# Two attention blocks of sixteen 8-feature heads, packed four side by side into TensorE's tiles

## The reference

```
scores = q @ k.T * 8 ** -0.5        (128 x 128; the fifth block adds a causal mask)
out    = softmax(scores) @ v        (128 x 8)
x      = x + concat(out) @ Wo + bo
```

## Time and profile before

| | us |
|---|---|
| median of 3 runs | 1275.42 (1272.52 to 1280.17) |
| the profiled execution | 1274.87 |
| its span | 1273.1 |
| first block, from the query product to the first scores | 10.57 to 49.25 |
| its head loop, to the turn of tokens | 49.25 to 129.14 |
| fifth block, from the product with `Wqkv` to the first scores | 383.18 to 418.46 |
| its head loop, to the turn of tokens | 418.46 to 539.45 |

### The profile page before, as it was taken

One profiled execution on the slowest core, in us unless ns is written; L12 is line 12 of the kernel. 1 busy time (PEld: TensorE's weight loads), 2 busy tenths in 40 slices (PEclk: granted clock), 3 DMA queues, 4 the chain that ended last, 5 costly groups with the idle time before them and its releaser, 6 DMA issues.

```text
span 1273.1 us, 18672 instructions
## 1 busy us (share of the span) xinstructions
PE 1145.1 (90%) x7950; PEld 769.5 (60%) x7950; DVE 549.3 (43%) x952; ACT 488.7 (38%) x755; POOL 423.3 (33%) x194
## 2 busy tenths in 40 slices
PE   7999798998989999988878986999999999999558
PEld 4898543673676788825556873655565565565334
DVE  2234466114436433354233334445554544553444
ACT  2355532433435544524343203444334434443111
POOL 0144111001000455401001000778677678677000
PEclk9799899996778999979997997999999999999769
DMA  8322100003000233210045102122123113110100
GB/s 338 128 101 117 51 33 34 1 1 148 34 15 19 88 130 133 117 67 33 17 194 220 67 14 119 67 91 108 67 68 132 67 66 133 67 67 1 72 1 9
DMA packets 20772, 102.96 MB, mean 81 GB/s; under 512 B 1744, under 2 KB 1744, under 8 KB 18896
## 3 DMA queue, kind: packets, MB, share of 16 engines
q1 hardware_dynamic: 20688, 101.75, 20.8%
HBM read 67.93 MB, written 33.82 MB: 80 GB/s over the span
## 4 chain that ended last, share of the span: by engine, by line
PE 83%; DVE 7%; ACT 5%; issue 2%; POOL 2%; DMA 0%; POOLq 0%; DVEq 0%; ACTq 0%
PE PSUM L2122 18%; PE PSUM L2048 10%; PE PSUM L1529 8%; PE PSUM L1662 4%; PE PSUM L1653 3%; PE PSUM L1539 3%; PE PSUM L1581 3%; PE PSUM L1618 3%; PE PSUM L1759 2%; PE PSUM L1770 2%; PE PSUM L1612 2%; PE PSUM L1714 2%; PE PSUM L2165 1%; PE PSUM L1981 1%; PE PSUM L1971 1%
## 5 line engine op out<-in xcount | busy, mean ns | idle before, releaser
L470 POOL TENSOR_TENSOR CK<-CK,ARENA 128x2048 f32<-128x2048 f32 x63 | 285.1, 4526 | 123.3 <-ACT ARENA L770 119.2
L2122 PE MATMUL PSUM<-ARENA,CT 128*128 128x512 f32 x512 | 238.7, 606 | 0.0
L1370 DVE TENSOR_TENSOR ARENA<-PSUM,RK 128x512 f32<-128x512 f32 x256 | 159.0, 684 | 183.8 <-PE PSUM L2048 183.8
L770 ACT ACTIVATE ARENA<-ARENA,WB 128x1024 f32<-128x1024 f32 x128 | 147.0, 1148 | 200.9 <-DVE ARENA L1370 198.2
L2122 PEld LDWEIGHTS PSUM<-ARENA,CT 128*128 128x128 f32 x512 | 91.4, 189 | 98.6 <-issue 90.5
L2048 PEld LDWEIGHTS PSUM<-ARENA 64*128 64x128 f32 x2048 | 119.4, 188 | 51.0 <-issue 47.0
L1529 PE MATMUL PSUM<-CT,WK 128*128 128x128 f32 x1024 | 144.6, 288 | 0.0
L1529 PEld LDWEIGHTS PSUM<-CT,WK 128*128 128x128 f32 x1024 | 129.8, 199 | 12.1 <-issue 8.7
L2048 PE MATMUL PSUM<-ARENA 64*128 64x128 f32 x2048 | 131.8, 278 | 2.7 <-ACT WB L765 2.2
L399 POOL TENSOR_TENSOR RSTD<-VE,MHALF 128x4 f32<-128x4 f32 x17 | 17.1, 1008 | 344.9 <-DVE VE L845 282.1
L413 POOL TENSOR_TENSOR W<-KEYS 128x512 f32<-128x512 f32 x28 | 36.8, 1314 | 126.5 <-ACT KEYS L493 92.6
(11 more groups left out here) (390 smaller groups left out, 1670.7 us busy)
## 6 DMA issues: line engine op xcount, KB each, us to landing
ARENA<-kept_keys SPq DMA_DIRECT2D x16, 2048.0 KB, 7.9
kept_keys<-KEYS SPq DMA_DIRECT2D x32, 512.0 KB, 2.6
kept_keys<-W SPq DMA_DIRECT2D x32, 512.0 KB, 2.6
CT<-in_ctxT SPq DMA_DIRECT2D x4, 1024.0 KB, 10.7
CK<-in_l0f_experts SPq DMA_DIRECT2D x1, 4096.0 KB, 22.5
CK<-in_ctxk SPq DMA_DIRECT2D x1, 4096.0 KB, 12.3
ARENA<-in_l2f_experts SPq DMA_DIRECT2D x2, 2048.0 KB, 7.8
CT<-in_ctxk SPq DMA_DIRECT2D x1, 4096.0 KB, 14.1
```

The lines of the kernel that those rows point to most:

```text
L470: nc.gpsimd.tensor_tensor(LS[b % 2], LS[b % 2], PR[:, t % 2, :], ALU.add)\
L770: act(p, p, ACT.Exp, bias=SHIFT).then_inc(sem("l3x_probs"), AC.sends("l3x_probs"))
L1370: ve.tensor_tensor(PR[:, k, q * 512:(q + 1) * 512].rearrange("p (j n) -> p j n", j=4), bank(q).rearrange("p (j n) -> p j n", j=4), each(rk ...
L2122: last = mm(bank(4 + q), CTK[:, t, :], PR[:, t % 2, q * 512:(q + 1) * 512], start=k == 0, stop=k == KEY_TILES - 1)
```

## The change

It changes both blocks in the same way.

- Heads lie in the array's quarters. Head j of a group has its 8 features in partitions 32j to 32j+7 for queries (`QH`) and keys (`KVH`), and its values in the 8 partitions behind. The four score products of a group use four row tiles and go to four banks (0 to 3), all of which the next group needs again: scores(g+1) waits until group g has been shifted.
- The product with the exponents is turned round: the 32-wide weights are the values, 8 columns that count, and a column of ones (`VH`) that gives the sum of the exponents. Four column tiles side by side fill a slice of bank 6; VectorE copies the bank every four groups (`keep_values`), so its sums (`total`) go. After the loop TensorE turns the kept values (`turn_values`, 16 transposes) and `normalize_heads` divides, with one reciprocal and one product for each batch element.
- Queries, keys and values are made by column-tiled products with 32-wide weights: in the first block 16 of 512 columns for the queries and 64 of 128 for keys with values; in the fifth 128 of 128 columns, whose moving operand is read in runs of 8 tokens. The masked copies of the queries, the transposes by heads, and the copies of 8 partitions go. Values get to rows by 16 transposes, and ScalarE copies them (`keep_value_rows`).
- GpSimd clears `VH` (2048 columns) and sets its ones ahead of each block (`value_pads`), directly behind the norm's power.
- The transposed exponents have one bank (4). A key tile has two banks where it had three: rows in 5 and 7, the sums of the tile before in 5 behind its first half of rows, the norms two tiles back in 7 ahead of its second half. The order of a tile is: turn norms of s-2, rows half 0, rows half 1, sums of s-1.
- The weights of the first block no longer wait for the array `wb`; `l3x_pick` has moved to `wa`.

```diff
-        VS = SM[:, 512:1024]
+        QH, KVH, VH, OH32 = (ARENA[:, k * 2048:(k + 1) * 2048] for k in range(4))
...
+            def value_pads():
+                nc.gpsimd.memset(VH, 0.0).then_inc(sem("value_pads"), PO.sends("value_pads"))
+                nc.gpsimd.wait_ge(sem("value_pads"), PO.sent("value_pads"))
+                nc.gpsimd.memset(VH.rearrange("p (h x) -> p h x", x=32)[:, :, 16:17], 1.0)\
...
+            def heads_act(place, scale):
+                first = places[place][0]
+                def begin(s):
+                    if s > first and s >= 2:
+                        keep_key_norms(s - 2, 7)
+                    keep_key_rows(s, 0, 5)
+                def end(s):
+                    if s:
+                        keep_key_sums(s - 1, 5)
+                for g, (one, two) in enumerate(key_steps(place)):
+                    nc.scalar.wait_ge(sem("scores_shifted"), AC.due("scores_shifted"))
+                    act(SX[:, g % 2, :], SX[:, g % 2, :], ACT.Exp, scale=scale).then_inc(sem("probs"), AC.sends("probs"))
...
+                        begin(one)
+                    if two is not None:
+                        keep_key_rows(one, 1, 7)
+                        end(one)
+                    nc.scalar.wait_ge(sem("probs_turned"), AC.due("probs_turned"))
...
+                    act(PT[:, g % 2, :], bank(4), ACT.Copy).then_inc(sem("pt_ready"), AC.sends("pt_ready"))
+                    if two is not None:
+                        begin(two)
+                        keep_key_rows(two, 1, 7)
+                        end(two)
+                    elif one is not None:
+                        keep_key_rows(one, 1, 7)
+                        end(one)
...
+            def normalize_heads():
+                for b in range(B):
+                    o = bank(b).rearrange("p (h x) -> p h x", x=32)
+                    nc.vector.wait_ge(sem("values_turned"), DV.due("values_turned"))
+                    ve.reciprocal(L_INV[:, b * H:(b + 1) * H], o[:, :, 16]).then_inc(sem("dve_step"), DV.sends("dve_step"))
+                    nc.vector.wait_ge(sem("dve_step"), DV.sent("dve_step"))
+                    last = ve.tensor_tensor(ACC[:, b, :].rearrange("p (h e) -> p h e", h=H), o[:, :, HD:2 * HD],
+                                            each(L_INV[:, b * H:(b + 1) * H], HD), ALU.mult)
...
+            for k in range(8):
+                rows_of = (QH, KVH)[k // 4].rearrange("p (c j) -> p c j", j=H)[:, :, 4 * (k % 4):4 * (k % 4) + 4]
+                bias = w(("l1a_bq", "l1a_bkv")[k // 4])[:, 4 * (k % 4):4 * (k % 4) + 4]
+                nc.vector.wait_ge(sem("kv_rows"), DV.due("kv_rows"))
+                ve.tensor_tensor(rows_of, bank(k).rearrange("p (j c) -> p c j", j=4), over(bias, P), ALU.add)\
...
                     for j in range(4):
-                        last = mm(PSUM[:, 1 + g % 2, j * P:(j + 1) * P], q_of(g, j), k_of(g, j), start=True, stop=True)
+                        r = slice(32 * j, 32 * j + HD)
+                        last = mm(PSUM[:, j, 0:P], q_of(g, r), KVH[r, g * P:(g + 1) * P], start=True, stop=True)
...
+                def begin(s):
+                    if s > first and s >= 2:
+                        nc.tensor.wait_ge(sem("keys_kept"), 2 * s)
+                        turn_norms(s - 2, 7)
+                    key_rows(s, 0, 5)
+                def end_rows(s):
+                    if s > first and s >= 2:
+                        nc.tensor.wait_ge(sem("key_norm_rows"), s - 1)
+                    key_rows(s, 1, 7)
+                def sums(s):
+                    if s:
+                        nc.tensor.wait_ge(sem("keys_kept"), 2 * s + 1)
+                        sum_squares(s - 1, 5)
...
                     for j in range(4):
-                        last = mm(out_of(g, j), PT[:, g % 2, j * P:(j + 1) * P], v_of(g, j), start=True, stop=True)
+                        last = mm(PSUM[32 * j:32 * j + 32, 6, (g % 4) * P:(g % 4 + 1) * P], VH[:, g * P + 32 * j:g * P + 32 * j + 32],
+                                  PT[:, g % 2, j * P:(j + 1) * P], start=True, stop=True, skip_group_check=True)
...
+            at_q = cols["l0x_WqT"][1]
+            for g in range(4):
+                for j in range(4):
+                    at = at_q + (4 * g + j) * HD
+                    last = mm(PSUM[32 * j:32 * j + 32, 1 + g, :], WA[:, at:at + 32], HT[:, :], start=True, stop=True)
...
+                    at, j = at_kv + h * 2 * HD, h % 4
+                    last = mm(PSUM[32 * j:32 * j + 32, (5, 6, 7, 0)[b], (h // 4) * P:(h // 4 + 1) * P], WA[:, at:at + 32], CTB[:, b, h, :],
...
+            ht = HT[:, :].rearrange("p (g r t) -> p r g t", r=4, t=8)
+            for k in range(8):
+                if k == 4:
+                    keys_settled(places["l1a_norm"][-1], places["l1a_norm"][-2])
+                for n in range(4):
+                    j = 4 * (k % 4) + n
+                    at = cols["l1a_Wqkv"][1] + (j * HD if k < 4 else P + j * 2 * HD)
+                    for r in range(4):
+                        last = mm(PSUM[32 * r:32 * r + 32, k, n * P:(n + 1) * P], WB[:, at:at + 32], ht[:, r, :, :],
```

## The result

The changed kernel takes **1203.66 us** (median of four runs, 1201.56 to 1204.03) against 1277.8 for the kernel before in the same comparison: a ratio of 0.942 (0.939 to 0.946). That is 9 us less than the forecast of 1213 and inside its range. The profiled execution took 1201.56 us with a span of 1199.8; the span fell by 73.3 us, and the forecast had 61.6.

The account below looks back on a forecast made before the run. TensorE was taken to bound the kernel. First block 20.5 - 2.5 + 10.7 - 3.0 = 25.7, fifth 21.7 - 2.3 + 21.4 - 4.9 = 35.9; 1274.9 - 61.6 = 1213 us, range 1198 to 1240.

Parts of the forecast that it names:

- Bound: Head loops of both blocks: TensorE is the limit, so work taken off it shortens them until a hand-over takes its place.
- Front of the first block: Before the first block's heads: group 2 ends at 45.5 us instead of 66.05, held by a queued transfer; 20.5 us gained.
- Clock behind the wait: First block, after TensorE idles some 6 us: the first 4 to 5 us run at half speed, 2.5 us lost.
- Head loop, first block: Period per group falls from 4.84 to 3.95 us; 12 groups gain 10.7 us.
- Head loop, fifth block: Two-tile groups fall from 8.27 to 6.8 us, one-tile groups from 5.1 to 4.15; 21.4 us gained.
- End of the first block: After the heads, added transposes and VectorE's normalization make the turn 3.0 us later; in the fifth block 4.9.
- Front of the fifth block: Before the fifth block's heads: 21.7 us gained, less 2.3 for GpSimd's 3.8 us clearing that slows VectorE's normalization.
- Between and behind: Everything between and behind the two changed blocks moves as it is, with no gain or loss of its own.
- The first: Rival: PSUM evacuations bind; 0.6 + 0.2 us for each of 43 key tiles, 34 us lost, 1247 us; chance 0.15.
- The second: Rival: the array's tiles run one behind another, 64 us lost, 1277 us, no change; chance 0.03.
- The third: Rival: the key tile's transfer isn't held by the queue and gaps are smaller, 1202 us; chance 0.15.
- The fourth: Rival: the clock stays at its lower level in both head loops, some 135 us more, 1348 us; chance 0.04.

Follow-up runs that it names:

- Experiment 1: Changed kernel with the experts' 4 MB load issued after the first block's 15 key tiles instead of ahead of them: 1193.06 us (median of four).
- Experiment 8: Changed kernel with TensorE repeating the second half of tile 2's rows eight times over in the first block's wait: 1195.26 us, on another chip.
- experiment 6: Changed kernel issuing, from each block's third group on, one score product and one transpose of probabilities instead of four each: 1208.42 us.
- experiment 3: Changed kernel with GpSimd clearing the value tile ahead of the first block's normalization instead of right behind its reciprocal root: 1203.71 us.
- experiments 4 and 5: Changed kernel with scores in one row strip (1210.72 us) or issued twice in four strips (1212.81 us, other chip); with values in one column strip (1219.82 us).
- the best version: Changed kernel with expert load behind the key tiles, bias row and two normalizations earlier, value clearing earlier, first rows earlier: 1191.85 us (median of six).

## Why the prediction was right, and where its sizes were off

The time was within the range and the mechanism that was forecast is the one in the trace. By its steps:

- **Bound.** TensorE bounds both loops. Held, but for some 0.13 us of each period in which it waits for ScalarE's copy of the sums.
- **Front of the first block.** Forecast: copies done at 25, ScalarE at tile 2's rows by 36, let go at 42.7 by a transfer stuck behind the experts, group 2 done at 45.5. Measured: first scores at 23.34, released at 42.58, 45.16. Experiment 1 showed that the experts' load is the cause, and the 13.5 us from issue to release that it is their order in the queue. Gain 20.9 against 20.5.
- **Clock behind the wait.** 2.5 us forecast. Measured 1.8 in group 3 (5.61 less 3.81) and 0.65 in the end of group 2, which the 45.16 above has in it. Experiment 8 showed the cause.
- **Head loop, first block.** 3.95 us forecast, 3.81 measured, so 12 groups gave 12.4 against 10.7. The values (0.24 for 0.3) and the turn (0.44 for 0.50) were cheaper, and the 0.1 of waiting for the probabilities didn't come; experiment 6 says by how little: another 0.09 us off TensorE would have met their copy. The other hand-over was mis-sized: 0.47 was forecast from the end of the sums' slot to the norms' turn, to be covered nearly whole by the scores. It is 0.56, and the scores cover 0.43 of it. Their own price was right: 0.28 of records and 0.2 of change forecast, 0.23 a round and about 0.2 measured.
- **Head loop, fifth block.** 6.8 forecast, 6.85 measured; with one tile 4.15 forecast (from 5.1; the subtraction there gives 5.4, the trace before has 5.13, 524.23 to 529.36), 3.81 measured. Together 22.2 us against 21.4. GpSimd's squares didn't become the wait.
- **End of the first block.** 3.0 later forecast. From the other terms (29.6 = 20.9 - 1.8 + 12.4 - x) it is 1.9. A reciprocal with its product took 0.49, not 0.6 (98.33 to 98.82), and 0.9 had been put down for a clock that stayed at 1.00 here (50 to 99 us). In the fifth block 4.9 was forecast for the end; the block from its first key rows on gained 17.9 (119.0 to 101.1), which leaves 4.3.
- **Front of the fifth block.** Here the forecast missed most: 24.0 gained, against 21.7 less 2.3. The step that failed is the clearing. It does block VectorE (2.37 us for the normalization, and experiment 3's 1.11 without it), but it lasts 1.80 and not 3.8: the rate was carried up from a clearing of 32 columns, and whatever is fixed in its 0.152 us was so counted 64 times. And TensorE is at key rows and sums until 350.01 while VectorE is held, so next to nothing was lost (10.16 us from the turn at 339.85 to that at 350.01, before 10.02), and the forecast hadn't asked what TensorE had in hand there. The other part: 256 records took 7.19 us, 0.028 each, where 0.036 from the short runs gave 9.1, and VectorE's additions took 0.69 (the lower bound) and not 1.0. The moving operand in runs of 8 columns cost nothing: the first block's 128 records on plain columns took 3.67, 0.029 each.
- **Between and behind.** "Moves as it is" was wrong by 2.2 us up to the fifth block and by -1.2 behind it. For 1.7 of the 2.2 that is the clock at the place shown above. For the rest the granted clocks point the same way (0.86 from 99 to 111 us, before 0.75 from 129 to 142; 0.66 from 465 to 480, before 0.76 from 539 to 553), but no run isolates it.

All in all: first block 29.6 against 25.7, fifth block 42.0 against 35.9, between them 2.2, behind them -1.2, and the last 0.7 of the span.

**The rivals.** The first (evacuations bind, 1225 to 1247) came true for one copy and a small part of its price: the copy of the sums binds by 0.13 us per key tile, where 0.8 was put down, and that of the probabilities was 0.09 away. The second (no overlap) is refuted by experiments 4 and 5 (0.43 us for four score products side by side, 1.09 in one strip; values 0.35 and 1.00). The third, at 1202, came nearest to the time by accident: the transfer was held by the queue in full; only its other half, smaller gaps, is there. The fourth (the lower clock throughout) didn't happen: the mean granted clock was 1.00 from 50 to 99 us and from 365 to 465.

## What to carry to other kernels

Price packed products by two numbers: what one round costs (here 0.23 us for four strips, as much as one further product in a strip) and what it costs to enter and leave the shape (about 0.2). Before you call a slot's length a price, look at what lets the instruction behind it go: here 0.56 us stayed with one product, with four and with none, because a copy of ScalarE held what followed. A group in which something else follows tells the two apart. When an edit brings a stage forward by 26 us, list the transfers that are queued ahead of its first store: here a load that nobody needed until 193 us cost 9 us of the first block, and moving one line gave them back. And read an edit of 1 to 3 us in the length of its own stretch: the end of this program moves by more than that with the clock.

## What the runs showed of the hardware that I had not expected

- A group's scores of 8 rows take 0.41 us with one product, 0.43 with four in four strips, 0.66 with eight in two rounds, and 1.09 with four in one strip.
- ScalarE's copy of 128 x 128 sums took 0.28 us, but from the start of the last eight sum records to the product that reads the copy it was 0.89 us, with work between them or without.
- A clearing of 2048 columns on GpSimd took 1.80 us, and 64 columns 0.24; beside the first four VectorE instructions of 128 columns took 2.37 instead of 1.11 us.
- After a wait of 8.3 us TensorE ran at 0.50 of its clock for another 5.5 us (43.72 to about 49.3). Useless products in the wait avoided that. Behind one and the same wait of 1.90 us the clock fell in one execution and not in another.
- Executions of one kernel differ with their mean granted clock: the best version's six spans were 1180.6 us at 0.939, 1186.2 and 1187.8 at 0.931, 1192.3 and 1192.7 at 0.927, and 1193.1 at 0.926, about 1 us for each thousandth. The changed kernel's four don't follow that: 1199.8 at 0.932, 1202.1 at 0.929, 1202.2 at 0.925 and 1201.6 at 0.923.
